# Eighteen start-up steps reordered: scores, maxima, inversions, the add of x, and the filler matmuls

## The reference

```
x = x + attention(lstm(x, h0))      # causal, 16 heads of 64, keys and values from a latent of 32
x = x + moe(gru(x, h0))             # 8 experts, best 2 of each token, hidden size 512, exact gelu
```

## Time and profile before

| what | before |
|---|---|
| time of the profiled execution | 553.72 us |
| its span, first to last instruction | 551.9 us |
| TensorE busy | 515.3 us, 93% of the span |
| VectorE busy | 437.2 us, 79% |
| ScalarE busy | 365.1 us, 66% |
| granted TensorE clock, mean | 0.969 of 2.4 GHz |
| first LSTM activation | 9.90 us |
| an undisturbed LSTM step (steps 1 to 3) | 1.77 us |
| first GRU activation | 61.99 us |

### The profile page before, as it was taken

How to read it: one execution, slowest core, us unless ns; L and a number is a source line. 1 busy time by engine, 2 the same in 40 slices (tenths; PEclk the granted TensorE clock), 3 DMA queues, 4 the chain that set the end, 5 groups by cost and what they waited for, 6 DMA issues and landing times.

```text
span 551.9 us, 20513 instructions
## 1 busy us (share of the span) xinstructions
PE 515.3 (93%) x7482; PEld 470.6 (85%) x7524; DVE 437.2 (79%) x2370; ACT 365.1 (66%) x1329; POOL 34.2 (6%) x89
## 2 busy tenths in 40 slices
PE   8979799899799999999999999999999999989997
PEld 3746567799679999999999999999999998879987
DVE  4556768779877988888888888888989888884776
ACT  2335454776366776767676767776767767777995
POOL 7000000000000000000000000000000000000000
PEclk9789989999959999999999999999999999999999
DMA  8910101001110101010202010101101010100000
GB/s 211 355 14 9 16 6 14 11 10 15 16 13 7 17 5 18 14 20 2 22 12 22 2 20 15 16 8 14 16 14 15 7 17 15 18 2 1 13 7 11
DMA packets 75120, 14.35 MB, mean 26 GB/s; under 512 B 71411, under 2 KB 74111, under 8 KB 74638
## 3 DMA queue, kind: packets, MB, share of 16 engines
q1 hardware_dynamic: 74566, 11.96, 12.0%
q10 hardware_dynamic: 456, 1.08, 0.6%
HBM read 7.78 MB, written 1.05 MB: 16 GB/s over the span
## 4 chain that ended last, share of the span: by engine, by line
PE 72%; DVE 14%; ACT 7%; issue 5%; DMA 0%; SPq 0%; DVEq 0%; ACTq 0%
PE pH L516 20%; PE pY L516 12%; PE pG L516 12%; PE pL L516 9%; PE pV L516 6%; PE pC L608 6%; PE pC L516 5%; PE pS L516 4%; ACT hid L910 3%; DVE latNlo L1040 1%; DVE acc L1136 1%; DVE mx L1046 1%; ACT PThi L899 1%; DVE ghi L1222 1%; DVE gB L1219 1%
## 5 line engine op out<-in xcount | busy, mean ns | idle before, releaser
L910 ACT ACTIVATE hid<-pH,b 128x256 f32<-128x256 f32 (+1 forms) x320 | 115.1, 453 | 0.0
L516 PE MATMUL pY<-w,hid 128*128 128x128 f32 (+1 forms) x656 | 80.9, 268 | 0.0
L516 PE MATMUL pH<-ghi,w1hi 128*128 128x256 f16 (+1 forms) x320 | 75.3, 252 | 2.4 <-ACT hid L910 1.7
L516 PE MATMUL pH<-ghi,w1lo 128*128 128x256 f16 (+1 forms) x320 | 75.5, 253 | 0.0
L516 PE MATMUL pH<-glo,w1hi 128*128 128x256 f16 (+1 forms) x320 | 75.5, 252 | 0.0
L516 PEld LDWEIGHTS pY<-w,hid 128*128 128x128 f32 (+1 forms) x656 | 70.6, 171 | 0.1
L921 ACT ACTIVATE gT<-pG 128x32 f32<-128x32 f32 x128 | 24.6, 192 | 57.1 <-PE pG L516 55.8
L899 ACT ACTIVATE PThi<-pC 128x512 f16<-128x512 f32 x64 | 38.1, 595 | 18.2 <-PE pC L608 18.2
L954 ACT ACTIVATE lC<-lT 128x16 f32<-128x16 f32 x128 | 28.0, 219 | 32.1 <-DVE lT L1234 31.7
L608 PE MATMUL pC<-ident,P 128*128 128x128 f32 x256 | 42.6, 291 | 6.6 <-DVE acc L1136 4.6
L516 PE MATMUL pG<-gRZ,gW 128*128 128x16 f32 x256 | 44.7, 250 | 4.1 <-DVE gRZ L1197 3.8
(11 more groups left out here) (188 smaller groups left out, 1653.7 us busy)
## 6 DMA issues: line engine op xcount, KB each, us to landing
w<-in_w SPq DMA_DIRECT2D x2, 2048.0 KB, 13.9
qbd<-qh SPq DMA_DIRECT2D x256, 16.0 KB, 1.9
out<-acc SPq DMA_DIRECT2D x16, 64.0 KB, 1.5
xT<-in_xT ACTq DMA_DIRECT2D x1, 960.0 KB, 7.7
hid<-in_WqT SPq DMA_DIRECT2D x1, 512.0 KB, 5.3
hid<-in_Wout SPq DMA_DIRECT2D x1, 512.0 KB, 9.9
lWh<-in_lWh SPq DMA_DIRECT2D x1, 256.0 KB, 2.8
lWx<-in_lWx SPq DMA_DIRECT2D x1, 256.0 KB, 3.2
```

The lines of the kernel that those rows point to most:

```text
L516: return nc.tensor.matmul(o, lhsT=lhsT, rhs=rhs, start=start, stop=stop, skip_group_check=True)
L910: A(hid[:, e % NHID, c, 0:W], pH[half][:, W * at:W * (at + 1)], ACT.Gelu, bias=b1[:, e, c:c + 1], scale=1.0 / SP).then_inc(gelu, 1)
```

## The change

Scores of a unit that fall before step 18 are issued a step later, straight behind `l_step`. Those of units 0 to 3 come at k = 11 to 14 instead of at the end of k = 10 to 13. From k = 18 on scores stand where they were.

On VectorE, before step 18, `maximum` and `invert` move behind the step's last LSTM operation. The maximum of a unit then falls in the same step as its scores.

In `after_latents`, `setup_late` goes last and `add_x` before `q_rest`. Before step 18 `q_rest` is done in the step of `lat_q` itself (k = 8 and 16) instead of a step later (9 and 17). From step 24 on it stays a step later, now behind `add_x`.

Fillers: the two groups of two in steps 7, 15 and 17 behind the products are left out (12 matmuls), and in steps 18, 19 and 20 two instead of four stand in for the missing values (6 matmuls).

```diff
                 if t < LAG:
                     l_step(t)
+                    if unit_at(k - 1, O_S) is not None:
+                        scores(unit_at(k - 1, O_S), k)
                     keep_warm(k, startup_fill(k))
...
                 elif LAG <= k < WARM_END:
-                    keep_warm(k, 4)
+                    keep_warm(k, 2 if k < LAG + 3 else 4)
...
-                if k < WARM_END and not (LAG <= k and t % GS == GS - 1):
+                if k < WARM_END and k != LAG - 1 and t % GS != GS - 1:
                     keep_warm(k, startup_fill(k))
-                if unit_at(k, O_S) is not None:
+                if unit_at(k, O_S) is not None and k >= LAG:
                     scores(unit_at(k, O_S), k)
-                if k < LAG:
+                if k < LAG and k != LAG - 1 and t % GS != GS - 1:
                     keep_warm(k, startup_fill(k))
...
             def after_latents(k):
-                setup_late(k)
                 if latents_at(k) is not None:
                     lat_copy(latents_at(k))
-                if latents_at(k - 1) is not None:
-                    q_rest(latents_at(k - 1))
                 if period_at(k) is not None:
                     add_x(period_at(k))
+                if latents_at(k) is not None and k < LAG:
+                    q_rest(latents_at(k))
+                if latents_at(k - 1) is not None and k > LAG:
+                    q_rest(latents_at(k - 1))
+                setup_late(k)
...
-                if unit_at(k - 1, O_S) is not None:
+                if unit_at(k - 1, O_S) is not None and k >= LAG:
                     maximum(unit_at(k - 1, O_S))
...
-                if unit_at(k, O_V) is not None and (k < LAG or k % TB):
+                if k >= LAG and unit_at(k, O_V) is not None and k % TB:
                     invert(unit_at(k, O_V))
...
                 if k < LAG:
+                    if unit_at(k - 1, O_S) is not None:
+                        maximum(unit_at(k - 1, O_S))
                     after_latents(k)
+                    if unit_at(k, O_V) is not None:
+                        invert(unit_at(k, O_V))
                     between(k)
```

## The result

The changed kernel takes 549.5 us (median of 20 runs, 547.14 to 553.58), the kernel before 554.08 in 20 runs beside them. The ratio is 0.9917, with a 95% interval of 0.9901 to 0.9933. The forecast of 546.5 had the direction right. 549.5 lies 0.5 us outside the narrow range that it held with 0.60 (543.5 to 549) and inside the widened one (542.5 to 551.5). 4.6 us came of the 7.3 it counted: 0.8% instead of the "over 1%" that it gave 0.74. The profiled executions differ by more, 547.90 against 553.72, or 5.8 us.

What follows compares the result with a forecast made beforehand. With TensorE busy 93%, the start of the GRU's first activation was taken to decide; terms summed to -7.3 us from the profiled 553.72, giving 546.5. Range 543.5 to 549 (held with 0.60), widened to 542.5 to 551.5.

Steps and rivals of the forecast that it cites:

- the signs named beforehand: Step 11 at 33.5 to 34.5, first GRU activation 54.5 to 56, 0.5 to 1.2 us waits before first two scores.
- the signs of being wrong: First GRU activation above 57, clock below 1 in over two stretches (50 to 100 us), or periods 0.2 us longer.
- fillers of step 7: Step 8's product waits behind four fillers on TensorE; removing them gives -0.85 us.
- queries' DMA out of the product's way: Step 11's product no longer waits for the queries' DMA, scores go behind it, low halves come at step 8: -4.5 us.
- given back in steps 11 to 15: Late maxima, exponentials and ScalarE's set-up copies slow these LSTM steps, at some 2.7 us each: +0.7 us.
- fillers of step 15: Step 16's product stands behind these fillers on TensorE; removing them gives -0.8 us.
- steps 16 and 17, x, gate fill: x added earlier despite a new VectorE wait, and four fillers before the first GRU product gone: -1.5 us.
- steps 18 to 20: Fewer fillers: 0.1 us in steps 18 and 19, 0.6 us in step 20; together -0.7 us.
- steps 21 to 27: Later-period order may lose 0.3 us at step 27, which has few products: +0.3 us.
- Step 16's new wait: VectorE's low halves wait for ScalarE's copy of the queries, so VectorE reaches step 17's operations 0.85 us late.
- The periodic order: Low halves behind x delay gB: nothing from step 33; rival 0.3 to 0.6 us a period, chance 0.04 slower, 0.06 mild.
- The rival "falls more often": With 18 fewer fillers TensorE's clock has more short falls and one more late fall: 550 to 551 us, chance 0.17.

Runs made afterwards that it cites:

- experiment 7: Changed kernel with the old order from step 18 on (set-up casts first, queries' low halves before x): 546.84 us, ratio to the kernel before 0.9854.
- experiment 9: Changed kernel with values out before the queries' low halves at step 16, and the old order from step 18 on: 545.59 us, ratio to the kernel before 0.9841.
- experiment 6: Changed kernel with one query DMA instead of four for each of units 0 to 3: 546.42 us, ratio to the kernel before 0.9847.
- experiment 1: Kernel before with only scores moved behind the next product, and maxima and inversions behind the LSTM's operations: 554.8 us, ratio 0.9984.
- experiment 2: Kernel before with only the queries' low halves moved to the step of their projection (8 and 16): 553.48 us, ratio 0.9965.
- experiment 3: Kernel before with only the fillers thinned, 18 fewer: 552.01 us, ratio 0.9945.
- experiment 4: Changed kernel with all fillers as before, 18 put back: 552.61 us, ratio to the kernel before 0.9960.
- experiment 10: Experiment 9's kernel with one filler instead of two at each place of steps 8 to 16: 545.57 us, ratio to the kernel before 0.9831.
- experiment 5: Changed kernel with the queries' low halves last on VectorE at steps 8 and 16, behind the values: 548.11 us, ratio to the kernel before 0.9863.
- experiment 8: Changed kernel with 16 fillers added in steps 41 to 44: 550.77 us, ratio to the kernel before 0.9898.
- experiment 11: Experiment 9's kernel without any fillers from step 18 on: 552.54 us.

## Why the prediction was right, and where it was too large

The direction and the way to it were right: a gain in the start-up, which arrives at the end whole. Of the signs named beforehand, step 11 (34.20 us) and the two waits before the scores (0.95 and 0.53) came. The first GRU activation at 56.38 is 0.4 outside its bounds, and steps 12 to 15 lie 2.4, 4.1 and 2.5 us apart instead of 2.6 to 2.8. The distances between GRU activations from step 53 on moved by more than 0.1 us at three single steps, 58, 74 and 90, by -0.36, +0.20 and +0.31. Of the signs of being wrong the last came, for two periods: steps 25 to 33 took 0.64 us longer, and steps 89 to 97 0.30, which they do with the old order of experiments 7 and 9 too (0.21 and 0.24). Shifts of the activations in the profiled pair, by the terms of the sum:

| term | predicted, us | measured in the profile, us |
|---|---|---|
| fillers of step 7 (steps 7 to 8) | -0.85 | -0.64 |
| queries' DMA out of the product's way (8 to 11) | -4.5 | -4.16 |
| given back in steps 11 to 15 | +0.7 | +1.67 |
| fillers of step 15 | -0.8 | -1.01 |
| steps 16 and 17, x, gate fill | -1.5 | -1.39 |
| steps 18 to 20 | -0.7 | -0.80 |
| steps 21 to 27 | +0.3 | +0.49 |
| the rest | 0 | +0.19 |
| sum, with -0.08 from before step 7 | -7.3 | -5.7 |

**The main term that was mis-sized is steps 11 to 15**: +0.7 forecast, +1.67 measured. I took landings 2.6 us apart, from SP's issues. Unit 2's four DMAs were issued on time, but landed 2.9 us after the issue instead of 1.9, and the scores waited 1.16 us. Experiment 6 shows the price, 1.1 us, and without that wait steps 11 to 15 take 11.55 us against the 11.01 of before: +0.5, near the 0.7 counted. So the late landing is the whole miss of this term. (The prediction reads 5.3 steps in the 15.00 us from 41 to 56; by the activations it is 5.2, which moves nothing.) The transfers of SP, changed kernel, 38 to 39 us (percentages are of the 16 engines; the last number is the time to landing):

```profile
q1 hardware_dynamic: 459, 0.03, 27.0%
q8 instruction: 1, 0.02, 7.6%
...
qbd<-qh SPq DMA_DIRECT2D x3, 16.0 KB, 2.9
```

A transfer of instructions (0.02 MB) falls there. In all thirteen profiles the slowest landings of this stretch, 2.6 to 3.2 us (median of the issues of one microsecond), stand beside such a transfer; in the kernel before at 43 to 44 us, where nobody waited. A smaller one (0.01 MB), which comes 1 to 4 us ahead of it, has landings of 1.9 to 2.3 us beside it in all but experiment 6. It is not the queries' own DMAs that crowd each other out: in experiment 6, with a quarter of them, the landing took 2.8 us too. That the transfer of instructions is the cause is likely and not shown: nothing was run that moves it.

**The DMA wait** was 0.3 us smaller in gain. In this execution the clock rose late: two fillers of step 8 took 0.89 us, and the chain of the queries began 0.4 us later than counted. Alone, neither half of this edit is worth what I gave it: scores behind the product bring at most 0.2 to 0.9 us (experiment 1), early low halves 1.5 to 1.9 (experiment 2); the 4.5 at step 11 shrinks by what the following steps and the clock take.

**Fillers** were forecast right in sum: 0.85 + 0.8 + 0.86 + 0.7 = 3.2 us, and experiments 3 and 4 measure 3.0 and 2.4 to 3.1. They are the largest part of what the change is worth. The 0.7 of steps 18 to 20 is the weak term. Steps 18 to 21 take 9.12 us in experiments 6, 9 and 10, where the clock stayed at 2.4 GHz, and 9.21 in experiment 4, with the old fillers at the same clock: 0.1 us. In the changed kernel, which takes 9.91 there, and in the kernel before (10.71) the clock fell in this stretch, so the 0.80 of the table meets the forecast for a reason that is in part the clock's.

**Step 16's new wait** was forecast at 0.85 us and costs 0.7 (experiment 5). **The periodic order** was costed at nothing from step 33 on, which holds: in step 97 gB starts 1.87 us behind the GRU's activation instead of 1.54, the 0.3 I counted, and the distances are as before but for three single steps, two of which (58 and 90) moved in experiments 7 and 9 too. For the one period with few products I allowed 0.3, and it costs 0.93 (experiment 7); the slack of the first scores, 1.3 us in step 98, is not there at step 26. That the table shows only +0.49 for steps 21 to 27 is luck: the kernel before had a fall of the clock at 81 to 86 us and took 22.16 us for these steps, where experiments 1, 2 and 3, the same code from step 21 on without that fall, took 21.57 to 21.74.

**The clock.** The rival "falls more often" did not come: time at 1.2 GHz went from 35.9 us on average (27 runs of before) to 32.2. The changed kernel's own 20 runs say what that is worth: five at a mean clock of 0.975 average 547.9 us, two at 0.963 average 552.9. The difference in clock is 13 us at 1.2 GHz, so each such microsecond goes with 0.38. That is no constant: in the stretch of experiment 8 it was 0.09 (0.9 us for 10), and between experiments 11 and 9 it was 0.15 (7.0 us for 46). By these prices the 3.7 us less at 1.2 GHz are an estimated 0.3 to 1.4 us of the gain, and the rest of it the order and the fillers. The profiled pair flatters the change: that execution of the changed kernel lies 1.6 us below its median, that of before 0.4 below its own, which is the 1.2 between 5.8 and 4.6. The prediction took its 1.8 between median and profile from three runs. Most of the changed kernel's runs had more time at 1.2 GHz than the profiled one. I bounded the clock by one late fall more or less, 544 to 549, and the median of the result lies 0.5 outside that.

## What to carry to other kernels

When an engine's wait moves off the recurrence's path, count what its later waits cost step by step, and the landing of each transfer at its worst seen, not its usual duration: 1.5 of the 4.9 us gained at step 11 were gone by step 14. Fillers that stood before a critical product cost 2.4 to 3.1 us in sum here and could go; those from step 18 on held the clock, and without them the kernel was 7 us slower. Tell the two apart in the trace and take out only the first kind. The new order of the loop was free where the experts' products covered it and cost 0.93 us where they did not, so look at the lightest iteration before taking it for all.

## What the runs showed that was not expected

- The clock differs between executions of one kernel, and with it the time: at equal code the mean clock ran from 0.963 to 0.975 and the time from 553.6 to 547.1 us. For changes of 1% the clock has to be listed beside each time.
- The clock fell in every profiled execution between about 136 and 169 us, for 17 us in one stretch in all but experiments 8 (6.8 us) and 10 (20.5 us). That TensorE counts as busy for 14.12 of the 15.00 us from 150 to 165 in the changed kernel is no contradiction: the clock was low by then, and a slower matmul is busy longer. Ahead of the fall it was busy for 2.66 of the 4.00 us from 140 to 144; with the fillers of experiment 8, for 3.93, and there the clock held.
- Experiments 4, 8 and 10 have one more fall, of 6.8 us between 484 and 498 us, and with it steps 135 to 138 take 12.5 us instead of 10.1. The other ten profiles, the kernel before and the changed one among them, have none there, so a single profile can be 2.4 us off for this alone.
- Leaving out the fillers from step 18 on more than doubled the time at 1.2 GHz, from 26.7 to 72.6 us.
- The time from issue to landing of the same 16 KB DMA is 1.9 us mostly, and 2.6 to 3.2 us beside a 0.02 MB transfer of instructions, in all thirteen profiles.
